# A graph layer in three turns a chunk, with its join in the same block

## The chip, the cores and the metric

The kernel runs on 1 core of a Trainium2 chip. The metric is the device time of one execution in microseconds (us); lower is better.

## The reference, cut to what matters

The program is four graph layers behind one another, each with a residual and a layer norm, over 50,000 nodes and 50,000 edges of 128 numbers. The change touches the first layer alone:

```python
def _L0_gnn_ref(x, edge_index, W, b, ln_gamma, ln_beta):
    h = x @ W
    loops = jnp.arange(N, dtype=edge_index.dtype)
    src = jnp.concatenate([edge_index[0], loops])
    dst = jnp.concatenate([edge_index[1], loops])
    deg = jax.ops.segment_sum(jnp.ones(src.shape, dtype=h.dtype), dst, num_segments=N)
    dinv = jnp.where(deg > 0, jax.lax.rsqrt(deg), 0.0)
    norm = dinv[src] * dinv[dst]
    out = jax.ops.segment_sum(h[src] * norm[:, None], dst, num_segments=N) + b
    mu = out.mean(axis=-1, keepdims=True)
    var = out.var(axis=-1, keepdims=True)
    out = (out - mu) * jax.lax.rsqrt(var + LN_EPS) * ln_gamma + ln_beta
    return jax.nn.relu(out)

x = _layernorm(x + _L0_gnn_ref(x, edge_index, ...), axis=-1)
```

## The kernel before, in words

The edges are sorted by their target. The first layer, `gcn` (L1407), takes them in 56 chunks (`k.NB`) of 7 columns (J) by 128 partitions. A chunk's tiles lie in rings: 8 slots (UB) for what is loaded and gathered, 4 (RING) for what is computed. The 7 columns go through TensorE in two groups, (0,4) and (4,7). All 56 chunks are unrolled. What is done for a chunk:

- SyncE loads the chunk's record (L1031): node and source indices, weights. `bring` (L1429) loads the source rows of the first few chunks and places words beside rows of a table.
- GpSimd, `fetch` (L1437): 14 indirect gathers, `own` (the node's own row, L1449) and `both` (the source row with two words, L1453; L1451 for the first few chunks), column by column.
- ScalarE, `weigh` (L1455): for each column one activation of the source row into `run` (L1466) and one of the own row into `summed` (L1467).
- VectorE, `edges` (L1470): 7 steps of a running sum over edges with one target (L1476), which sets `edged`; then 7 steps that add it to the own rows (L1478), which sets `prepped`.
- SyncE, `keep` (L1482): the running sums and the source words go to memory.
- TensorE: transposes (L1068); ScalarE copies (L1109); product with the folded weight (L1074 with the bias, L1080); ScalarE copies to `z` (L1117).
- VectorE, `stats` of z (L781 to L784, L777); ScalarE, logarithm and exponent, `log` (L791, L793); VectorE, `root` (L800 to L804); ScalarE, `first.apply` (L812, y<-z).
- VectorE, `residual` (L1499): scale, bias, relu and own row in three wide steps (L1502 to L1504), which sets `freed`, the release of the chunk's slot; then the second norm's stats. Then second log, second root, and on ScalarE `apply` and `apply_twice` (L812, out<-y): two normalised outputs. The latter's end is `finished`.
- SyncE, store (L1042 to L1046): both outputs to memory.

`Flow.run` (L1007) walks over turns u = −5 to 58 and gives each engine a hand-written list of (lag, stage):

- VectorE: edges of chunk u+3, stats of u, residual of u−1, first root of u, second root of u−1.
- ScalarE: copy of one group, weigh u+4, second apply (both outputs) u−2, copy of one group; then first log u, second log u−1, first apply u, copies.
- SyncE: load u+5 (waits for `freed` of the chunk 8 earlier), keep u+1 (waits for `edged`), store u−3 (waits for `finished`). So the load of chunk c stands behind the store of c−9.
- GpSimd: the gathers of one chunk after another, each chunk as soon as its record is there and its source words of 8 chunks earlier are kept.

Behind the last turn the block ends. A second block (L1541 to L1591) joins the running sums across the 128 partitions: GpSimd clears and gathers three small tiles, TensorE joins and transposes, one row per partition goes through the product and three small norms (`RowNorm`, L1168: VectorE, with GpSimd's power at L1185), and two scatters write the rows. The next stage begins with a table load on ScalarE (L2083).

Of the kernel before, what the change touches and what calls it, by code (L numbers as in the profile page):

```python
# [17 lines left out]
D = 128  # L18
J = 7
# [37 lines left out]
def wait(eng, sem, value, passed=None):  # L57

    if isinstance(value, int) and value <= 0:
        return  # L60
    eng.wait_ge(sem, value)
    if passed is not None and not isinstance(value, int):
        eng.sem_inc(passed, 1)


class Chain:
# [5 lines left out]
    def at(self, chunk):  # L72
        self.base, self.n = chunk * self.per, 0
# [1091 lines left out]
class RowNorm:  # L1165
# [7 lines left out]
        self.asked, self.rooted = k.semaphore(f"row_asked{i}"), k.semaphore(f"row_rooted{i}")  # L1173

    def run(self, dve, step, v, o):
        step(dve.bn_stats(out=self.raw[:], in_=v))
        step(dve.bn_aggr(out=self.mv[:], in_=self.raw[:]))
        step(dve.tensor_scalar(self.mv[:, 1:2], self.mv[:, 1:2], self.eps, None, ALU.add))
        dve.nop().then_inc(self.asked, 1)
        dve.wait_ge(self.rooted, 1)  # L1180
        step(dve.tensor_scalar(o, v, self.mv[:, 0:1], self.mv[:, 1:2], ALU.subtract, ALU.mult))

# [224 lines left out]
def gcn(k):  # L1407
# [3 lines left out]
    with ExitStack() as c:  # L1411
# [43 lines left out]
        def weigh(act, c):  # L1455

            i = c.slot(UB)
            if plain(c):
                act.wait_ge(xs_in[i], (c.use(UB) + 1) * 16)
            n.wait_got(act, c)  # L1460
            n.wait_rec(act, c)
            wait(act, edged, c.count(1, 2 - RING))
            wait(act, put_out[c.slot(RING)], c.use(RING) * 16)
            wait(act, n.turned, c.count(NG, (1 - RING) * NG))
            for j in range(J):
                act.activation(R(run, c)[:, j, :], xs[:, i, j, :], ACT.Copy, scale=where[:, i, j, 1:2])  # L1466
                ins = act.activation(R(summed, c)[:, j, :], own[:, i, j, :], ACT.Copy, scale=n.field(c, OWN2)[:, j : j + 1])  # L1467
            ins.then_inc(weighted, 1)

        def edges(dve, step, c):  # L1470

            r = c.slot(RING)
            dve.wait_ge(weighted, c.count(1, 1))
            for j in range(J):
                prev = run[:, r, j - 1, :] if j else run[:, (r - 1) % RING, J - 1, :]
                step(dve.scalar_tensor_tensor(run[:, r, j, :], prev, n.field(c, SAME)[:, j : j + 1], run[:, r, j, :], ALU.mult, ALU.add))  # L1476
            dve.nop().then_inc(edged, 1)
            step(*[dve.scalar_tensor_tensor(summed[:, r, j, :], run[:, r, j, :], n.field(c, OWN1)[:, j : j + 1], summed[:, r, j, :],  # L1478
                                            ALU.mult, ALU.add) for j in range(J)])
            dve.nop().then_inc(n.prepped, 1)  # L1480

        def keep(sp, c):  # L1482

# [5 lines left out]
        def kept(sp):  # L1489
            for u in range(RING):  # L1490
                sp.wait_ge(put_out[u], k.NB // RING * 16)
            for u in range(UB):
                sp.wait_ge(src_out[u], k.TN * 16)

        def stats(dve, step, c):
            n.wait_z(dve, c)
# [8 lines left out]
            dve.nop().then_inc(n.freed, 1)  # L1505
            second.stats(dve, step, c, v)

        def apply_second(act, c):
            n.wait_stored(act, c)
            act.wait_ge(src_out[c.slot(UB)], (c.use(UB) + 1) * 16)  # L1510
            second.apply(act, c, R(y, c), R(n.o[0], c))
            second.apply_twice(act, c, R(y, c), R(n.o[1], c))

        side = Prepare(k, c, [n.p_t[0][0], n.p_t[1][0], *n.p_m], [y, n.z, n.o[0]])

        def begin(dve):
            side.vector(dve)
            step = Chain(dve, begun)
            step(dve.memset(run[:, RING - 1, J - 1, :], 0.0))

            step(dve.memset(n.o[1][:, :, :, 0:1], 1.0))

        n.z_free = first.applied
        n.finished, n.freed = second.applied2, sem("freed")
        n.n_got = 2
        cut = 1
        n.run([], [], [k.res, k.tab[1]], lambda c: [R(summed, c)], [k.w_skip],
              [(3, edges), (0, stats), (-1, residual), (0, first.root), (-1, second.root)],
              [(4, weigh), (-2, apply_second), (0, first.log), (-1, second.log), (0, lambda act, c: first.apply(act, c, R(n.z, c), R(y, c)))],
              [], prep=True, sp_stages=[(1, keep)], begin=begin, sp_end=kept,  # L1530
              pe_begin=side.tensor, sp_after={-4: side.bring, UB - 1: side.put_away}, fetch=fetch, bring=bring, cut=cut)
# [5 lines left out]
        cleared, fetched, joined, done, summed1 = [sem(x) for x in ("cleared", "fetched", "joined", "jdone", "summed1")]  # L1537
        turned1, copied1, made1, ready, put = [sem(x) for x in ("turned1", "copied1", "made1", "ready", "put")]
        p_j, p_t, p_z = n.p_t[0][0], n.p_t[1][0], n.p_m[0]
        dinv = hint[:, 1:2]  # L1540
        with nc.Block(no_gpsimd_drain=True) as b:  # L1541

            @b.gpsimd
            def _(pool):
                pool.memset(head[:], 0.0).then_inc(cleared, 1)
                pool.wait_ge(cleared, 1)
                pool.indirect_dma_start(head[:], None, k.runs, bass.IndirectOffsetOnAxis(ap=k.join_row[:], axis=0),
                                        bounds_check=k.NR - 1, oob_is_err=False).then_inc(fetched, 16)
                pool.indirect_dma_start(mine[:], None, A["x"], bass.IndirectOffsetOnAxis(ap=k.head_node[:], axis=0)).then_inc(fetched, 16)
                pool.indirect_dma_start(hint[:].bitcast(I32), None, k.info, bass.IndirectOffsetOnAxis(ap=k.head_node[:], axis=0)).then_inc(fetched, 16)  # L1550
                for norm in norms:
                    norm.root(pool)
                pool.wait_ge(ready, 1)
                for table, tile in ((k.res, z), (k.tab[1], o)):
# [5 lines left out]
            def _(pe):  # L1560
                pe.matmul(p_j[:, 0:D], k.join_t[:], run[:, RING - 1, J - 1, :], start=True, stop=True).then_inc(joined, 1)
                pe.wait_ge(summed1, 1)
                pe.transpose(p_t[:, 0:D], o[:], k.ident[:]).then_inc(turned1, 1)
                pe.matmul(p_z[:, 0:D], k.ones_bf[:], k.b_rows[:, 0, :], start=True, stop=False)
                pe.wait_ge(copied1, 1)
                pe.matmul(p_z[:, 0:D], ot[:], k.w_skip[:], start=False, stop=True).then_inc(made1, 1)

            @b.scalar
            def _(act):
                act.wait_ge(turned1, 1)  # L1570
                act.activation(ot[:], p_t[:, 0:D], ACT.Copy).then_inc(copied1, 1)

            @b.vector
            def _(dve):
                step = Chain(dve, done)
                dve.wait_ge(fetched, 48)
                step(dve.tensor_scalar(o[:], mine[:], dinv, None, ALU.mult))
                dve.wait_ge(joined, 1)
                step(dve.tensor_tensor(o[:], o[:], p_j[:, 0:D], ALU.add))
                step(dve.tensor_tensor(o[:], o[:], head[:], ALU.add))  # L1580
                step(dve.tensor_scalar(o[:], o[:], dinv, None, ALU.mult))
                dve.nop().then_inc(summed1, 1)
                dve.wait_ge(made1, 1)
                norms[0].run(dve, step, p_z[:, 0:D], z[:])
# [180 lines left out]
class RowPieceNorm:  # L1765
# [1516 lines left out]
```

## Time and profile before

| | us |
|---|---|
| median of 3 runs | 7949.5 (7933.11 to 7982.95) |
| the profiled execution | 7911.97 |
| its span, first to last instruction | 7910.2 |
| busy: PE / DVE / ACT / POOL | 5034.4 / 5379.6 / 4770.6 / 3828.5 |

The span holds four layers. The first layer's chunks lie between 516 and 1867 us. PE is TensorE, DVE VectorE, ACT ScalarE, POOL GpSimd, SPq SyncE's DMA queue. In the timelines the first number is the start, the second the duration; what stands in brackets is how long the engine was idle before and what ended that.

### The profile page before, as it was taken

Reading aid. Unit: us, or ns where it says so; the run is one execution under the profiler, and the core shown is the slowest. Engines: PE = TensorE matmul, PEld = TensorE weight load, DVE = VectorE, ACT = ScalarE, POOL = GpSimd, SP = SyncE. Lnnn points to the kernel's source line nnn. Section 1 sums busy time; section 2 is a strip of 40 time slices with the busy share of each in tenths; the row PEclk is TensorE's granted clock in tenths of the full one; section 3 lists DMA queues with packets and bytes.
Section 4 is the critical chain, followed back from the end, with each engine's and each line's share of the span. In section 5 each row is a group of like instructions: output and inputs, shape, how many; then the busy total and the mean of one; then the engine's idle time right before and its main releaser. Section 6 shows DMA issues by size and latency. Waiting matters only on the chain. (4 is left out here: it accounts for less than half of the span.)

```text
span 7910.2 us, 117580 instructions
## 1 busy us (share of the span) xinstructions
PE 5034.4 (64%) x28601; PEld 3898.2 (49%) x28601; DVE 5379.6 (68%) x27204; ACT 4770.6 (60%) x14264; POOL 3828.5 (48%) x3878
## 2 busy tenths in 40 slices
PE   4032222223888886878867888865787758777774
PEld 1021111122776674666756666653454546555553
DVE  7835556564777774777766887883555777777788
ACT  6025666563677684767766777782333556666665
POOL 3055555543555534444435445425553444655565
PEclk9555555555889897998888888887888989888887
DMA  9284444433566653444434555553443883333332
GB/s 176 30 49 104 96 105 97 95 96 103 166 180 181 172 164 111 145 145 151 149 129 123 165 161 157 164 144 119 144 152 119 288 272 112 120 118 118 121 126 75
DMA packets 608007, 1075.90 MB, mean 136 GB/s; under 512 B 263700, under 2 KB 370015, under 8 KB 607193
## 3 DMA queue, kind: packets, MB, share of 16 engines
q1 hardware_dynamic: 476056, 787.63, 31.8%
q0 software_dynamic: 129920, 280.46, 16.8%
q8 instruction: 231, 3.78, 0.2%
q14 instruction: 456, 3.73, 0.2%
q10 hardware_dynamic: 1344, 0.30, 0.0%
HBM read 564.38 MB, written 530.59 MB: 138 GB/s over the span
## 5 line engine op out<-in xcount | busy, mean ns | idle before, releaser
L1975 POOL DMA_INDIRECT xs<-tab,rec x1176 | 1177.5, 1001 | 700.7 <-DVE cA L2191 412.2
L2191 DVE CUSTOM_DVE_ANT_0 junk<-p_y,xs 128x129 f32<-128x129 f32 x2352 | 586.0, 286 | 716.8 <-PE p_y L2030 248.6
L2026 PE MATMUL p_a<-w_all,xt 128*128 128x128 f32 x2352 | 545.6, 316 | 493.1 <-ACT xt L2092 322.0
L2030 PE MATMUL p_y<-w_all,xt 128*128 128x258 f32 x2352 | 796.6, 424 | 91.2 <-DMA got<-in_x,idx 35.9
L2109 ACT ACTIVATE z<-p_a 128x384 f32<-128x384 f32 x1176 | 574.6, 489 | 411.1 <-PE p_a L1866 245.7
L2101 ACT ACTIVATE st<-xs,cb 128x128 f32<-128x128 f32 x2352 | 810.0, 398 | 4.4 <-DMA xsrc<-got 4.0
L2226 DVE SCALAR_TENSOR_TENSOR st<-st,cg 128x128 f32<-128x128 f32 x2352 | 717.1, 346 | 126.6 <-ACT st L2101 74.3
L2092 ACT ACTIVATE xt<-p_t 128x256 f32<-128x256 f32 (+1 forms) x1221 | 450.0, 369 | 571.1 <-DMA both<-x_info,rec 228.6
L1449 POOL DMA_INDIRECT in<-in_x,rec x392 | 380.3, 970 | 768.9 <-DMA rec<-meta 652.7
L1074 PE MATMUL p_m<-b_rows,ones_bf 3*128 3x512 bf16 x224 | 102.8, 459 | 947.9 <-issue 397.8
L2026 PEld LDWEIGHTS p_a<-w_all,xt 128*128 128x128 f32 x2352 | 386.6, 207 | 602.6 <-ACT xt L2092 403.6
L1973 POOL DMA_INDIRECT xd<-tab,rec x336 | 336.9, 1003 | 616.3 <-DMA rec<-meta 432.6
L2846 POOL DMA_INDIRECT xs<-res,rec x392 | 386.2, 985 | 446.7 <-PE p_t L2871 183.8
L1870 PE MATMUL p_m<-w_all,z 128*128 128x128 f32 x2352 | 500.6, 297 | 77.8 <-issue 48.8
L1142 POOL DMA_INDIRECT in<-tab,rec x392 | 400.3, 1021 | 304.2 <-DMA rec<-meta 191.4
L2047 PE MATMUL p_m<-w_all,xt 128*128 128x128 f32 x2352 | 522.8, 306 | 0.0
L1074 PEld LDWEIGHTS p_m<-b_rows,ones_bf 3*128 3x128 bf16 x224 | 21.3, 95 | 1014.0 <-issue 434.5
L887 ACT ACTIVATE o<-y,norm 128x127 f32<-128x127 f32 (+1 forms) x1176 | 512.2, 486 | 6.8 <-DVE norm L881 6.6
L1871 PE MATMUL p_m<-w_all,z 128*128 128x128 f32 x2352 | 487.9, 291 | 0.0
L1866 PE MATMUL p_a<-ident,st 128*128 128x128 f32 x2352 | 484.7, 290 | 4.2 <-DVE st L2226 2.3
L2849 POOL DMA_INDIRECT out<-o,nodes x392 | 407.9, 1040 | 158.3 <-issue 117.7
L2030 PEld LDWEIGHTS p_y<-w_all,xt 128*128 128x128 f32 x2352 | 400.3, 213 | 108.7 <-issue 101.8
(784 smaller groups left out, 16742.9 us busy)
## 6 DMA issues: line engine op xcount, KB each, us to landing
states<-st SPq DMA_DIRECT2D x168, 910.0 KB
own<-tab SPq DMA_DIRECT2D x168, 448.0 KB
tab<-o SPq DMA_DIRECT2D x168, 448.0 KB
runs<-run SPq DMA_DIRECT2D x112, 448.0 KB
tab<-out SPq DMA_DIRECT2D x112, 448.0 KB
x<-tab SPq DMA_DIRECT2D x112, 448.0 KB
xd<-tab SPq DMA_DIRECT2D x168, 192.0 KB
angles<-st SPq DMA_DIRECT2D x56, 532.0 KB
```

Source lines behind the costliest of these rows:

```text
L887: ins = act.activation(o[:, r, skip:], v[:, r, skip:], ACT.Identity, bias=s[:, 1, r : r + 1], scale=s[:, 0, r : r + 1])
L1866: ins = pe.transpose(p_a[i][:, h * D : (h + 1) * D], halves(a)[:, h, :], k.ident[:])
L1870: pe.matmul(out_, a[:, 0:D], k.w_val[:, 0, :], start=False, stop=False)
L1871: return pe.matmul(out_, a[:, D : 2 * D], k.w_val[:, 1, :], start=False, stop=final)
L1975: pool.indirect_dma_start(xs[:, i, j, 0:D], None, table, bass.IndirectOffsetOnAxis(ap=rec[:, i, SRC, j : j + 1], axis=0)).then_inc(got_in[ ...
L2026: ins = pe.matmul(p_a[two(own_c, own_i)][:, 2 * D : 3 * D], xt[:, four(c, i), D : 2 * D], k.w_own[:, D : 2 * D], start=True, stop=True)
L2030: ins = pe.matmul(p_y[two(c, i)][:, 0 : H * X1], xt[:, four(c, i), 0:D], k.w_qk[:], start=True, stop=True)
L2047: pe.matmul(out_, xt[:, (four(c, j) + SCORE * J + 1) % 4, D : 2 * D], k.w_own[:, 0:D], start=False, stop=False)
L2101: ins = act.activation(state_of(r, j)[:, h, :], xs[:, c.slot(UB), j, 0:D], ACT.Copy, scale=co.b[:, c.slot(2), h, j : j + 1])
L2109: act.activation(z[:, c.slot(2), j, :], p_a[two(c, j)][:, 0 : 3 * D], ACT.Copy).then_inc(st_copied, 1)
L2191: ins = dve.tensor_tensor_reduce(junk[:, two(c, j), h], p_y[two(c, j)][:, h * X1 : (h + 1) * X1], xs[:, c.slot(UB), j, :], scale, 0.0, ALU ...
L2226: ins = dve.scalar_tensor_tensor(mine[:, h, :], prev[:, h, :], co.g[:, c.slot(2), h, j : j + 1], mine[:, h, :], ALU.mult, ALU.add)
```

## The change

The first layer is no longer run by `Flow.run`; its lists stand in `gcn`. Chunk i takes three turns: VectorE does edges, stats and first root of i in turn i, and residual and second root of i−1 in it; ScalarE does second apply of i−2. `weigh` is split: source rows first, then the logarithm of the first norm of i−1, then own rows (`weigh_own`). `edges` goes group by group, and sets `prepped` for each. SyncE loads i+5, keeps i, stores i−2. The join moves into the same block: GpSimd's small gathers go behind the last chunk's, VectorE's join arithmetic stands between the last first root and the last residual. `RowNorm.run` becomes `ask` and `take`.

```diff
+        def weigh_own(act, c):
+            for j in range(J):
+                ins = act.activation(R(summed, c)[:, j, :], own[:, c.slot(UB), j, :], ACT.Copy, scale=n.field(c, OWN2)[:, j : j + 1])
+            ins.then_inc(own_weighted, 1)
...
         def edges(dve, step, c):
...
+            for a, z_ in GROUPS:
+                for j in range(a, z_):
+                    prev = run[:, r, j - 1, :] if j else run[:, (r - 1) % RING, J - 1, :]
+                    step(dve.scalar_tensor_tensor(run[:, r, j, :], prev, n.field(c, SAME)[:, j : j + 1], run[:, r, j, :], ALU.mult, ALU.add))
+                if z_ == J:
+                    dve.nop().then_inc(edged, 1)
+                if a == 0:
+                    dve.wait_ge(own_weighted, c.count(1, 1))
+                step(*[dve.scalar_tensor_tensor(summed[:, r, j, :], run[:, r, j, :], n.field(c, OWN1)[:, j : j + 1], summed[:, r, j, :],
+                                                ALU.mult, ALU.add) for j in range(a, z_)])
+                dve.nop().then_inc(n.prepped, 1)
...
+            @b.sync
+            def _(sp):
...
+                for i in range(k.NB + 2):
+                    if i + LEAD < k.NB:
+                        load(at(i + LEAD))
+                    if i < k.NB:
+                        keep(sp, at(i))
+                    if i == UB - 1:
+                        side.put_away(sp)
+                    if i >= 2:
+                        store(at(i - 2))
...
             @b.gpsimd
             def _(pool):
+                for i in range(k.NB):
+                    fetch(pool, at(i))
                 pool.memset(head[:], 0.0).then_inc(cleared, 1)
+                pool.indirect_dma_start(mine[:], None, A["x"], ...).then_inc(hinted, 16)
+                pool.indirect_dma_start(hint[:].bitcast(I32), None, k.info, ...).then_inc(hinted, 16)
                 pool.wait_ge(cleared, 1)
+                for u in range(RING):
+                    pool.wait_ge(put_out[u], k.NB // RING * 16)
...
             @b.tensor
             def _(pe):
...
+                for i in range(k.NB):
+                    for g in range(NG):
+                        turn(at(i), g)
+                    for g in range(NG):
+                        product(at(i), g)
...
             @b.scalar
             def _(act):
...
+                for i in range(k.NB + 2):
+                    c0, c1, c2 = at(i), at(i - 1), at(i - 2)
+                    if c0.there:
+                        weigh(act, c0)
+                    if c1.there:
+                        first.log(act, c1)
+                    if c0.there:
+                        weigh_own(act, c0)
+                    if c1.there:
+                        first.apply(act, c1, R(n.z, c1), R(y, c1))
+                    if c0.there:
+                        carry_turned(c0, 0)
+                    if c2.there:
+                        n.wait_stored(act, c2)
+                        act.wait_ge(src_out[c2.slot(UB)], (c2.use(UB) + 1) * 16)
+                        second.apply(act, c2, R(y, c2), R(n.o[0], c2))
+                    if c0.there:
+                        carry_turned(c0, 1)
+                    if i == k.NB:
+                        act.wait_ge(turned1, 1)
+                        act.activation(ot[:], p_t[:, 0:D], ACT.Copy).then_inc(copied1, 1)
+                    if c2.there:
+                        second.apply_twice(act, c2, R(y, c2), R(n.o[1], c2))
+                    if c0.there:
+                        for g in range(NG):
+                            carry_product(c0, g)
+                    if c1.there:
+                        second.log(act, c1)
...
             @b.vector
             def _(dve):
...
+                for i in range(k.NB):
+                    c0, c1 = at(i), at(i - 1)
+                    stage(s_edges, c0, edges)
+                    stage(s_residual, c1, residual)
+                    stage(s_stats, c0, stats)
+                    stage(s_second, c1, second.root)
+                    stage(s_first, c0, first.root)
```

## Rows read from the trace of the kernel before

**Rows 1.** The page's chain of work that ended last, share of the span
```profile
DVE 7%; PE 4%; ACT 2%; another core or an unknown queue 2%; issue 1%; POOL 0%; DMA 0%; SPq 0%; DVEq 0%; ACTq 0%; POOLq 0%
```
**Rows 2.** Timeline: VectorE's first edges, the join block, the next stage's start
```profile
516.30 2.68 DVE L1476 SCALAR_TENSOR_TENSOR run<-run,rec 128x128 f32<-128x128 f32 x7
...
1842.01 0.43 SPq L1045 DMA_DIRECT2D tab<-out  x1
1845.92 0.20 POOL L1545 MEMSET head<- 128x128 f32 x1 [114.38 <-POOLq L1022]
...
1862.36 1.05 POOL L1555 DMA_INDIRECT res<-z,join_row  x1 [1.39 <-DVEq L1591]
...
1867.41 1.28 ACT L2083 ACT_TABLE_LOAD   x1 [13.41 <-PEq L124]
```
**Rows 3.** Waits from 600 to 1700: us in total, times, longest
```profile
POOL in L1449 <- DMA rec<-meta: 285.2, 33, 18.0
...
ACT guess L793 <- DMA xsrc<-got: 67.8, 19, 4.7
```
**Rows 4.** Timeline of SyncE's queue, stores of the first output
```profile
600.63 0.32 SPq L1045 DMA_DIRECT2D res<-out  x1
...
1160.78 0.32 SPq L1045 DMA_DIRECT2D res<-out  x1
...
1177.61 0.32 SPq L1045 DMA_DIRECT2D res<-out  x1
...
1305.45 0.32 SPq L1045 DMA_DIRECT2D res<-out  x1
...
1326.73 0.32 SPq L1045 DMA_DIRECT2D res<-out  x1
...
1707.45 0.32 SPq L1045 DMA_DIRECT2D res<-out  x1
```
**Rows 5.** Timeline of VectorE, one turn after GpSimd's last gather
```profile
1769.72 0.17 DVE L800 TENSOR_TENSOR newton<-guess 128x14 f32<-128x14 f32 x1 [0.33 <-DVE norm L804]
...
1771.08 2.68 DVE L1476 SCALAR_TENSOR_TENSOR run<-run,rec 128x128 f32<-128x128 f32 x7 [0.34 <-DVE norm L804]
...
1776.15 1.45 DVE L781 BATCH_NORM_STATS2 raw<-z 128x6 f32<-128x128 f32 x7 [0.33 <-DVE summed L1478]
...
1778.82 1.09 DVE L1502 TENSOR_TENSOR y<-y,ln_g 128x896 f32<-128x896 f32 x1 [0.33 <-DVE rad L777]
...
1785.06 0.17 DVE L800 TENSOR_TENSOR newton<-guess 128x7 f32<-128x7 f32 x1 [0.33 <-DVE rad L904]
...
1786.36 0.17 DVE L800 TENSOR_TENSOR newton<-guess 128x14 f32<-128x14 f32 x1 [0.33 <-DVE norm L804]
```
**Rows 6.** Timeline of GpSimd, first and last of 28 gathers
```profile
1164.91 0.95 POOL L1449 DMA_INDIRECT in<-in_x,rec  x1 [5.04 <-DMA rec<-meta]
...
1199.69 0.94 POOL L1453 DMA_INDIRECT both<-x_info,rec  x1 [0.30 <-issue]
```
**Rows 7.** Stretch: us; busy PE, PEld, DVE, ACT, POOL; clock, DMA share, GB/s
```profile
1179.00:1204.00 25.00, 5.30 (x22) 4.17 (x21) 4.28 (x24) 10.10 (x30) 16.45 (x18) 0.50 0.48 98
```
**Rows 8.** Timeline of ScalarE in that stretch
```profile
1195.24 0.39 ACT L1466 ACTIVATE run<-both 128x128 f32<-128x128 f32 x1
...
1200.79 0.49 ACT L812 ACTIVATE out<-y,norm 128x128 f32<-128x128 f32 x1 [0.98 <-issue]
```
**Rows 9.** Waits of SyncE's queue from 600 to 1700
```profile
SPq L1031 <- DVEq L1505: 67.1, 14, 9.5
```
**Rows 10.** Groups by shape, 600 to 1700: busy us, mean ns, idle before
```profile
L1068 PE MATMUL p_t<-ident,summed 128*128 128x128 f32 x322 | 87.6, 420 | 0.0
```
**Rows 11.** Timeline of ScalarE, the undisturbed turn of rows 5
```profile
1772.56 0.47 ACT L1109 ACTIVATE xt<-p_t 128x384 f32<-128x384 f32 x1
1772.93 5.48 ACT L812 ACTIVATE out<-y,norm 128x128 f32<-128x128 f32 x14
...
1784.81 0.21 ACT L791 ACTIVATE guess<-rad 128x14 f32<-128x14 f32 x1 [5.11 <-DVEq L785]
```

More of the change, by code:

```diff
@@ L1175, in run, with ask @@
     def run(self, dve, step, v, o):
+        self.ask(dve, step, v)
+        self.take(dve, step, v, o)
+    def ask(self, dve, step, v):
         step(dve.bn_stats(out=self.raw[:], in_=v))
@@ L1179, in run, with take @@
         dve.nop().then_inc(self.asked, 1)
+    def take(self, dve, step, v, o):
         dve.wait_ge(self.rooted, 1)
@@ L1465, in weigh @@
             for j in range(J):
-                act.activation(R(run, c)[:, j, :], xs[:, i, j, :], ACT.Copy, scale=where[:, i, j, 1:2])
-                ins = act.activation(R(summed, c)[:, j, :], own[:, i, j, :], ACT.Copy, scale=n.field(c, OWN2)[:, j : j + 1])
+                ins = act.activation(R(run, c)[:, j, :], xs[:, i, j, :], ACT.Copy, scale=where[:, i, j, 1:2])
             ins.then_inc(weighted, 1)
+        def weigh_own(act, c):
+            for j in range(J):
+                ins = act.activation(R(summed, c)[:, j, :], own[:, c.slot(UB), j, :], ACT.Copy, scale=n.field(c, OWN2)[:, j : j + 1])
+            ins.then_inc(own_weighted, 1)
         def edges(dve, step, c):
@@ L1473, in edges @@
             dve.wait_ge(weighted, c.count(1, 1))
[L1474 to L1480, printed above, removed]
+            for a, z_ in GROUPS:
[9 more added lines that the diff above has]
+                dve.nop().then_inc(n.prepped, 1)
         def keep(sp, c):
@@ L1506, in residual @@
             second.stats(dve, step, c, v)
[L1508 to L1512, printed above, removed]
-        side = Prepare(k, c, [n.p_t[0][0], n.p_t[1][0], *n.p_m], [y, n.z, n.o[0]])
[L1516 to L1521, printed above, removed]
+        side = Prepare(k, c, [n.p_t[0][0], n.p_t[1][0], *n.p_m], [y, n.z, n.o[0]])
         n.z_free = first.applied
         n.finished, n.freed = second.applied2, sem("freed")
[L1525 to L1531, printed above, removed]
+        n.n_got, n.n_out = 2, 2
+        outs = [k.res, k.tab[1]]
+        at = lambda i: Chunk(k, i // UB, i % UB)
         head, mine, hint, o, ot, z = [sb(x, s) for x, s in (("head", [P, D]), ("mine", [P, D]), ("hint", [P, 2]), ("o", [P, D]),
@@ L1536, in gcn @@
         norms = [RowNorm(k, c, i) for i in range(3)]
-        cleared, fetched, joined, done, summed1 = [sem(x) for x in ("cleared", "fetched", "joined", "jdone", "summed1")]
+        own_weighted = sem("own_weighted")
+        cleared, hinted, fetched, joined, done, summed1 = [sem(x) for x in ("cleared", "hinted", "fetched", "joined", "jdone", "summed1")]
         turned1, copied1, made1, ready, put = [sem(x) for x in ("turned1", "copied1", "made1", "ready", "put")]
-        p_j, p_t, p_z = n.p_t[0][0], n.p_t[1][0], n.p_m[0]
+        p_j, p_t, p_z = side.sets[1][0:3]
@@ L1540, in gcn, with load, store @@
         dinv = hint[:, 1:2]
         with nc.Block(no_gpsimd_drain=True) as b:
+            @b.sync
+            def _(sp):
+                def load(c):
+                    wait(sp, n.freed, c.count(1, 1 - UB), n.passed)
+                    sp.dma_start(n.rec[:, c.slot(UB)].rearrange("p f j -> p (f j)"),
+                                 k.meta[:, c.n].rearrange("p f j -> p (f j)")).then_inc(n.rec_in[c.slot(UB)], 16)
+                    bring(sp, c)
+                def store(c):
+                    wait(sp, n.finished, c.count(1, 1), n.passed)
+                    for i, table in enumerate(outs):
+                        sp.dma_start(rows(table)[:, c.n, :],
+                                     n.o[i][:, c.slot(RING)].rearrange("p j d -> p (j d)")).then_inc(n.stored[c.slot(RING)], 16)
+                for i in range(LEAD):
+                    load(at(i))
+                    if i == 1:
+                        side.bring(sp)
+                for i in range(k.NB + 2):
[8 more added lines that the diff above has]
+                for u in range(RING):
+                    sp.wait_ge(n.stored[u], k.NB // RING * 16 * n.n_out)
+                    sp.wait_ge(put_out[u], k.NB // RING * 16)
+                for u in range(UB):
+                    sp.wait_ge(src_out[u], k.TN * 16)
@@ L1543, in _ @@
             @b.gpsimd
             def _(pool):
+                for i in range(k.NB):
+                    fetch(pool, at(i))
                 pool.memset(head[:], 0.0).then_inc(cleared, 1)
+                pool.indirect_dma_start(mine[:], None, A["x"], bass.IndirectOffsetOnAxis(ap=k.head_node[:], axis=0)).then_inc(hinted, 16)
+                pool.indirect_dma_start(hint[:].bitcast(I32), None, k.info, bass.IndirectOffsetOnAxis(ap=k.head_node[:], axis=0)).then_inc(hinted, 16)
                 pool.wait_ge(cleared, 1)
+                for u in range(RING):
+                    pool.wait_ge(put_out[u], k.NB // RING * 16)
@@ L1553, in _ @@
                 pool.wait_ge(ready, 1)
+                for u in range(RING):
+                    pool.wait_ge(n.stored[u], k.NB // RING * 16 * n.n_out)
                 for table, tile in ((k.res, z), (k.tab[1], o)):
@@ L1560, in _, with turn, product @@
             def _(pe):
+                def turn(c, g):
+                    a, z_ = GROUPS[g]
+                    pe.wait_ge(n.prepped, c.count(NG, g + 1))
+                    wait(pe, n.copied, c.count(NG, g - 1))
+                    for r in range(a, z_):
+                        ins = pe.transpose(n.p_t[g][0][:, (r - a) * D : (r - a + 1) * D], R(summed, c)[:, r, :], k.ident[:])
+                    ins.then_inc(n.turned, 1)
+                def product(c, g):
+                    a, z_ = GROUPS[g]
+                    wait(pe, n.z_in, c.count(NG, g - 1))
+                    pe.matmul(n.p_m[g][:, 0 : (z_ - a) * D], k.ones_bf[:], k.b_rows[:, 0 : z_ - a, :].rearrange("p r d -> p (r d)"),
+                              start=True, stop=False)
+                    pe.wait_ge(n.copied, c.count(NG, g + 1))
+                    for r in range(z_ - a):
+                        ins = pe.matmul(n.p_m[g][:, r * D : (r + 1) * D], n.xt[:, g, 0, r * D : (r + 1) * D], k.w_skip[:], start=False,
+                                        stop=r == z_ - a - 1)
+                    ins.then_inc(n.made, 1)
+                side.tensor(pe)
+                for i in range(k.NB):
[3 more added lines that the diff above has]
+                        product(at(i), g)
+                pe.wait_ge(edged, k.NB)
                 pe.matmul(p_j[:, 0:D], k.join_t[:], run[:, RING - 1, J - 1, :], start=True, stop=True).then_inc(joined, 1)
+                pe.matmul(p_z[:, 0:D], k.ones_bf[:], k.b_rows[:, 0, :], start=True, stop=False)
                 pe.wait_ge(summed1, 1)
                 pe.transpose(p_t[:, 0:D], o[:], k.ident[:]).then_inc(turned1, 1)
-                pe.matmul(p_z[:, 0:D], k.ones_bf[:], k.b_rows[:, 0, :], start=True, stop=False)
                 pe.wait_ge(copied1, 1)
@@ new lines, in carry_product @@
+                def carry_product(c, g):
+                    a, z_ = GROUPS[g]
+                    act.wait_ge(n.made, c.count(NG, g + 1))
+                    if g == 0:
+                        wait(act, n.z_free, c.count(1, 1 - RING))
+                    act.activation(n.z[:, c.slot(RING), a:z_, :].rearrange("p j d -> p (j d)"),
+                                   n.p_m[g][:, 0 : (z_ - a) * D], ACT.Copy).then_inc(n.z_in, 1)
+                for i in range(k.NB + 2):
[26 more added lines that the diff above has]
+                        second.log(act, c1)
@@ L1573, in _, with stage @@
             @b.vector
             def _(dve):
+                side.vector(dve)
+                begin = Chain(dve, begun)
+                begin(dve.memset(run[:, RING - 1, J - 1, :], 0.0))
+                begin(dve.memset(n.o[1][:, :, :, 0:1], 1.0))
+                s_edges, s_residual, s_stats, s_second, s_first = [
+                    Steps(dve, sem(x), n.passed) for x in ("d_edges", "d_residual", "d_stats", "d_second", "d_first")]
+                def stage(step, c, what):
+                    if c.there:
+                        step.at(c)
+                        what(dve, step, c)
+                        step.end()
@@ L1582, in _ @@
                 dve.nop().then_inc(summed1, 1)
+                stage(s_residual, final, residual)
                 dve.wait_ge(made1, 1)
-                norms[0].run(dve, step, p_z[:, 0:D], z[:])
+                norms[0].ask(dve, step, p_z[:, 0:D])
+                stage(s_second, final, second.root)
+                norms[0].take(dve, step, p_z[:, 0:D], z[:])
                 step(dve.tensor_tensor(z[:], z[:], k.ln_g[:], ALU.mult))
```

19 lines of the change are left out of this document (9 added, 10 removed).

## The prediction

> **What bounds the kernel now.** The chain of waits comes first: it is shared out thinly, VectorE leading with 7% [rows 1], so no single engine is the answer and the stage has to be read by itself. The change touches only the first layer, which runs from about 516 us (when VectorE is done with the weights) to 1867.41, where the next stage's table load starts [rows 2].
>
> The waits of that stretch show GpSimd idle 285.2 us for the record of the next chunk [rows 3]. It is not short of time: it waits for a load that stands in SyncE's queue right behind a store. So I read SyncE's stores next [rows 4]. From 600.63 to 1707.45 lie 46 turns, 24.06 us each, but they are not alike: 16.83 from 1160.78 on, 21.28 from 1305.45 on, and others must be far longer.
>
> What would a turn cost without disturbance? After GpSimd's last gather VectorE goes from second root to second root in 16.64 us (1769.72 to 1786.36), without a pause longer than 0.34: second root and its hand-over 1.36, edges 5.07, stats 2.67, residual 6.24, first root 1.30 [rows 5]. There the turn is VectorE's. The other 7.4 us come with GpSimd's gathers.
>
> GpSimd's rows show it: 28 gathers without a pause from 1164.91 to 1200.63, 1.28 each, so 17.5 to 18 a chunk [rows 6]. From 1179 to 1204, while this run lasts, VectorE is busy 4.28 of 25 us and ScalarE 10.10 [rows 7]. ScalarE shows what a slow stretch looks like: 14 weighings begin at 1195.24 and are over before 1200.79, under 0.4 us each, and there one row of 0.49 us stands behind 0.98 us of nothing [rows 8]. Of the 38 unbroken runs of gathers in the stage 25 are one chunk long and 13 two. A run of one chunk costs the others little, some 3.6 us at its tail, where ScalarE's second step of the logarithm stands (67.8 in 19 cases [rows 3]); a run of two costs the 25 us of that window. I take it that about 14 us of unbroken gathering sets the slow stretch off and a pause ends it; the trace shows the order in time, not the cause.
>
> Whether two chunks run together is a race. A store at 1160.78 lets GpSimd start at 1164.91, 4.13 later; the next store at 1177.61 is 12.7 into that run, its load lands before the run ends, and the runs join. The store at 1326.73 followed its forerunner by 21.28, so it came some 17 into its run: it was itself held until the run was nearly over, and the runs stayed apart.
>
> **The change, part by part.**
> *Loads and stores.* Today load c stands behind store c−9 and waits for the release of slot c−8; that wait cost 67.1 us in 14 cases, 4.8 each [rows 9]. In the new order load c stands behind store c−8, whose chunk has released its slot long before. The wait goes: 67.1/46 = −1.46 a turn at most. What is late next is the gather itself: it starts earlier, which can make two runs join where the wait kept them apart. Keep moves one place as well: SyncE's keep of the running sums now waits for the edges of the same turn, and behind it stand the store and the next load; these wait for the second apply, later in the same turn, so it holds up nothing.
>
> *VectorE's turn.* Same operations. Edges go in two groups, each with its own hand-over: between nothing and two pauses of the 0.34 that stand ahead of edges, 0.68; I take 0.36, so 17.0 a turn [rows 5].
>
> *The chain across the engines.* It now closes within one turn, where the old order gave it five. From the start s of edges: the first four columns are ready at s+2.9 (8 of 14 steps of 5.07), PE's four transposes at 0.42 [rows 10] take 1.3 to 1.7, ScalarE copies 0.5, applies the second norm once (7 rows, half of 5.48) 2.7, copies 0.5, applies it again 2.7 [rows 11]: the chunk two back is finished at s+10.8. Two more copies make z ready at s+11.7. VectorE's edges and residual take 5.4 + 6.2, so it gets there at s+11.7 as well: between nothing and 0.6 us of new wait for z, I take 0.3. A turn is 17.3, 0.66 over today's floor. Own rows are weighed in the second half of the old weighing, 2.0 us, while VectorE does first root and the first four run steps: hidden. ScalarE today waits 5.11 for stats in the undisturbed turn [rows 11]; this slack pays for the new waits. If the cover of the own rows is gone, the turn gets up to 2.0 longer. The first logarithm moves between the two weighings, just as stats end: nothing either way, up to 0.5.
>
> *GpSimd* has the same 14 gathers a chunk. *The start:* the first store comes in turn 2: 516 + 2×17.3 + 10.8 = 561, plus one slow stretch while GpSimd rushes: 15 (0 to 24); I take 576.
>
> *The end and the join.* Today 160 us lie between the store at 1707.45 and the next stage; the join block alone starts at 1845.92 [rows 2]. New: 47 turns behind the first store the last load goes out; then a turn with gathers (24), five at the floor (86), the drain of the last chunk: 6.3 to the end of first root, 2.7 apply, 6.2 residual, 1.9 logarithm and root, 5.4 second apply = 22.5. The join's own arithmetic and its two gathers lie beside that. What stays behind the last store: its landing, 3.9 (1842.01 to 1845.92), and the two scatters to the next stage, 5.05 (1862.36 to 1867.41), so 9 at least; 13 with the queues in between. If the join's cover were gone it would cost its 16 us again (1845.92 to 1862.36). Sum 145, against 160.
>
> *Sum:* the next stage starts at 576 + 47T + 145 = 721 + 47T, T the mean turn under gathers. Even with today's 1867.4 at T = 24.4. The sum hangs on T.
>
> *T.* 24.06 today, −1.46 for the release, +0.66 for the floor, and a loss in the slow stretches: ScalarE could run 14 weighings ahead there (from 1195.24 on), some 4 us of work for later turns; in the new order it can weigh only half of it before it needs VectorE, which is the slowest. 4 over three turns is 1.3; between 0 and that, 0.7. T = 24.0.
>
> 721 + 47×24.0 = 1849: −18 us. The profiled run had 7911.97 (span 7910.2), the median of three is 7949.5; the 18 us are taken from the median: **7931 us**.
>
> **The Trainium skill against the rows.** "SBUF — State Buffer", section "Who interferes with whom", says that a DMA never contends with a compute engine and that ScalarE's ports are shared with nobody. By it the gathers could not slow ScalarE, and the stalls would come from waits in the old order; the time would be that of rival C. Rows 8 speak against it, as ScalarE shows pauses there that no engine's release ends. No row shows which resource is short.
>
> **The rivals.**
> *A, runs stay apart:* the store comes 14 us or more into each run, is held to its end, and the next run starts afresh. For: the floor rises by 0.66, and ScalarE's in-order list makes the chunk finish late in the turn; s+10.8 plus 4.1 gives a run start, and the next finish is 17.3 − 4.1 = 13.2 in, only 0.8 short. It is self-holding: each tail costs some 4 us, so the next finish is late as well. Against: 13.2 is below 14. A turn is then 21.3 (1305.45 to 1326.73): 721 + 47×21.3 = 1722, −145: 7804.
>
> *B, slower:* every run joins with the next, in pairs, as no release wait parts them, and the tight chain advances in the slow stretch only as fast as VectorE, 4.28 of 25 us. From the store at 1177.61 to the stretch are 1.4 us, and it ends at 1204, 3.4 behind the run: 17.3 − 1.4 − 4.3 = 11.6 of the turn are left then, so the store comes 15.0 behind the run and the next run 4.1 later. Pair: 35.7 + 15.0 + 4.1 = 54.8, T = 27.4, +141: 8091. With ScalarE's 10.10 in place of 4.28 it is 49.0, T = 24.5, and nothing is lost. It decides from T = 26.1 (under 6.9 us get through); between that and 27.4 I take 26.7, +108: 8058. For: 13.2 lies near the 12.7 at which runs joined. Against: GpSimd restarted late after each pair today, and a single run followed.
>
> *C, no slow stretches:* T is the gathers' own 17.5: 721 + 823 = 1544, −324: 7626. Only if their cause is the order of the old queue.
>
> *D, the change brings only the end:* T stays at 24.06 because release, floor and lost advance cancel. 1852, −15: 7934. It is the forecast's neighbour and shares its chance.
>
> **How the numbers follow.** 1% is 79 us, about what a measurement of this kernel can tell from no change. Forecast with D, T from 22.7 to 26.1: 0.42 (range by itself 7870 to 8029). A 0.32, C 0.04: faster 0.36. B 0.22. The mixture can settle between A and B, so the range takes A with a margin down to T = 20.8 (7780) and B up to 26.7 (8058, rounded to 8060); left out are C and the outer halves of B and a few cases of A, 0.2.
>
> **What would show it.** Right: gather runs of 35 us still alternating with runs of 17 to 18, the release wait behind the record's load gone, VectorE's undisturbed turn 17.0 to 17.6 with a short wait for z before stats, the next stage's table load some 145 us behind the store that frees the last load. A: nearly all runs single and turns of 20.5 to 22. B: hardly a single run, two stores every 52 us or more. Wrong: an undisturbed turn over 18 (the chain, not VectorE, would be the bound), slow stretches under single runs, or a join that stands alone behind the last store.

## The result, and the profile after

The changed kernel is slower: 8050.14 us median (8031.36 to 8056.98, 4 runs) against 7941.31 (7912.96 to 7982.95, 4 runs) beside it, ratio 1.0144, interval 1.0111 to 1.0177. The forecast was 18 us shorter; it came out 109 us longer, as rival B had it. That B's +108 is met so closely is partly luck: only 81 us of the difference lie in the edited layer, as the next lines show.

The profiled executions differ by 119.5 us (spans 8029.7 and 7910.2). 81.3 of these lie in the first layer, whose end is the next stage's table load: 1948.71, before 1867.41 [rows 2]. The other 38 lie in stages that were not edited; the kernel before differs by 70 us between its own four runs, so no cause is given for them here. By the three terms of the sum:

| | forecast | before | after |
|---|---|---|---|
| first store | 576 | 600.63 | 597.05 |
| mean of the next 47 turns | 24.0 | 24.08 | 25.72 |
| from that store to the next stage | 145 | 135.0 | 142.9 |
| next stage starts | 1849 | 1867.4 | 1948.7 |

The turn makes +77, the end +8, the start −4. SyncE's stores and loads in the timeline of the changed kernel show what became of the turn:

```profile
1149.33 0.32 SPq L1546 DMA_DIRECT2D res<-out  x1
...
1166.57 0.32 SPq L1546 DMA_DIRECT2D res<-out  x1
...
1203.77 0.32 SPq L1546 DMA_DIRECT2D res<-out  x1
...
1220.73 0.32 SPq L1546 DMA_DIRECT2D res<-out  x1
```

Turns of 17.2, 37.2 and 17.0: that is the pattern nearly throughout. GpSimd's gathers in the same stretch, the first of a run, the last of it, and the first of the next:

```profile
1153.41 0.94 POOL L1455 DMA_INDIRECT in<-in_x,rec  x1 [17.85 <-DMA rec<-meta]
...
1187.86 0.94 POOL L1459 DMA_INDIRECT both<-x_info,rec  x1 [0.30 <-issue]
...
1208.40 0.94 POOL L1455 DMA_INDIRECT in<-in_x,rec  x1 [19.61 <-DMA rec<-meta]
```

The run begins 4.1 behind the store at 1149.33. The next store comes 13.2 into it, its load lands as the first chunk's gathers end (a pause of 0.68), and the run goes on to 1188.80: 35.4 us, two chunks. The stores then stop until 1203.77, and GpSimd restarts 4.6 later: 55.0 us for two chunks, where rival B had 54.8. Behind the pair the turn is 17.0 again (1220.73), 12.3 into the new run, so that one is joined as well.

Not every pair is gathered without a break. Behind the opening there are 12 unbroken runs of two chunks and 26 of one, where the kernel before had 13 and 25. But 11 pairs of the single runs are only 0.7 to 2.1 us apart, and behind ten of these eleven comes a turn of 30 us or more, just as behind an unbroken run. Counted in this way the changed kernel has 23 pairs, the kernel before 14 (13 unbroken, one with a pause of 0.9). In this text two chunks are joined when no more than some 2 us part them.

What a turn is worth without and within a slow stretch, by the busy time of the engines (us; PE, PEld, DVE, ACT, POOL) in two stretches of the changed kernel:

```profile
1168.00:1192.00 24.00, 0.00 (x0) 0.00 (x0) 3.53 (x23) 5.38 (x19) 15.55 (x17) 0.55 0.30 85
1193.00:1210.00 17.00, 6.57 (x23) 4.55 (x23) 14.21 (x61) 14.99 (x43) 1.29 (x2) 0.50 0.25 84
```

In 24 us TensorE does nothing and VectorE 3.53 us of work; five us behind the run a whole turn takes 17. ScalarE no longer gets ahead there: 5.38 busy, before 10.10 [rows 7]. Not all of this idle time is of one kind:

```profile
1165.14 1.65 PE L1607 MATMUL p_m<-w_all,xt 128*128 128x128 f32 x6
...
1177.35 0.49 ACT L1641 ACTIVATE z<-p_m 128x384 f32<-128x384 f32 x1 [10.33 <-DMA idx<-in_src]
...
1187.84 0.23 DVE L804 SCALAR_TENSOR_TENSOR norm<-mean,norm 128x14 f32<-128x14 f32 x1 [1.23 <-issue]
...
1196.25 1.11 PE L1597 MATMUL p_t<-ident,summed 128*128 128x128 f32 x4 [29.46 <-DVEq L1495]
```

ScalarE stands 10.33 us although the product that it copies ended at 1166.79; the transfer that the profile names as the releaser started in the first 7 us of the execution. VectorE's small steps then follow one another with pauses of mostly 1.2 to 1.9 us for which the profile names no other engine, and ScalarE waits 8.41 us for them. TensorE only waits for VectorE's edges, so its zero does not show that it is slowed itself.

VectorE's undisturbed turn in the timeline (edges, stats, second root, first root, next edges) answers to [rows 5]:

```profile
1193.45 1.52 DVE L1488 SCALAR_TENSOR_TENSOR run<-run,rec 128x128 f32<-128x128 f32 x4 [0.34 <-DVE norm L804]
...
1198.76 1.09 DVE L1511 TENSOR_TENSOR y<-y,ln_g 128x896 f32<-128x896 f32 x1 [0.33 <-DVE summed L1493]
...
1204.99 1.46 DVE L781 BATCH_NORM_STATS2 raw<-z 128x6 f32<-128x128 f32 x7 [0.33 <-DVE rad L904]
...
1207.66 0.17 DVE L800 TENSOR_TENSOR newton<-guess 128x14 f32<-128x14 f32 x1 [0.33 <-DVE rad L777]
...
1209.01 0.17 DVE L800 TENSOR_TENSOR newton<-guess 128x7 f32<-128x7 f32 x1 [0.33 <-DVE norm L804]
...
1210.40 1.51 DVE L1488 SCALAR_TENSOR_TENSOR run<-run,rec 128x128 f32<-128x128 f32 x4 [0.34 <-DVE norm L804]
```

16.95 from edges to edges, with no pause for z. Edges take 5.31, before 5.07: the second group costs 0.24.

SyncE's waits from 600 to 1700, all of some size: the release wait of [rows 9] is gone, and keep now waits for edges.

```profile
SPq L1500 <- DVEq L1490: 567.6, 26, 31.1
SPq L1546 <- ACT out L812: 126.8, 24, 6.8
```

The first edges start at 534.40, 18 us later than before [rows 2], and the last store, the scatters and the next stage follow one another as forecast:

```profile
534.40 1.51 DVE L1488 SCALAR_TENSOR_TENSOR run<-run,rec 128x128 f32<-128x128 f32 x4
...
1939.14 0.32 SPq L1546 DMA_DIRECT2D res<-out  x1
...
1943.64 1.06 POOL L1586 DMA_INDIRECT res<-z,join_row  x1 [5.41 <-DMA tab<-out]
...
1948.71 1.28 ACT L2209 ACT_TABLE_LOAD   x1 [9.60 <-PEq L124]
```

### The profile page after: what moved, and what is told of

Its sections match the earlier page's. It is cut to its first block and busy times, and to the rows that moved or that the text cites. A ratio compares the mean times of both kernels' runs of the same rounds, so it can differ in the third digit from the quotient of the medians.

```text
span 8029.7 us, 117738 instructions
## 1 busy us (share of the span) xinstructions
PE 5080.1 (63%) x28601; PEld 3918.6 (49%) x28601; DVE 5384.2 (67%) x27204; ACT 4773.6 (59%) x14264; POOL 3811.8 (47%) x3878
## 5 line engine op out<-in xcount | busy, mean ns | idle before, releaser
L1597 PE MATMUL p_t<-ident,summed 128*128 128x128 f32 x392 | 113.0, 437 | 1019.6 <-DVEq L1495 777.2
L1597 PEld LDWEIGHTS p_t<-ident,summed 128*128 128x128 f32 x392 | 68.2, 215 | 1058.1 <-DVEq L1495 793.7
```

## The experiments

Theory J: two chunks gathered in one run cost the time, and whether runs join is a race of the next store against the run. Theory C: the chain closed within three turns is slow by itself. Times are medians in us; they are compared with the kernel before on the same chip, since its own median was 8043, 8040 and 7955 on the three chips used.

**a_noown: fewer gathers.**
```diff
-                pool.indirect_dma_start(own[:, i, j, :], None, A["x"], mine).then_inc(n.got[i], 16)
...
+                    sp.dma_start(own[:, c.slot(UB)].rearrange("p j d -> p (j d)"),
+                                 A["x"][0 : P * J, :].rearrange("(p j) d -> p (j d)", p=P)).then_inc(own_in[c.slot(UB)], 16)
```


> The changed kernel without the gather of own rows: each chunk loads the same 896 rows of x in one plain load instead, so 7 gathers a chunk are left out. J: runs of 9 us, far under the onset, a pause behind each; no slow stretch, every turn 16.9 to 17.3 as behind the last gather, first layer 350 to 410 us shorter, time 7640 to 7720. C: turn 20 or more even so. If the stores or plain loads make the slow stretch, it stays, as there are more of them.

The kernel leaves out the gathers of the chunks' own rows. 7579.2 in its one run. The mean turn is 17.02, nearly all of the turns 16.9 to 17.5; the runs are 8.4 to 9.4 us long. The stores, 16.87 and 16.96 apart:

```profile
1093.49 0.32 SPq L1548 DMA_DIRECT2D res<-out  x1
1110.36 0.32 SPq L1548 DMA_DIRECT2D res<-out  x1
1127.32 0.32 SPq L1548 DMA_DIRECT2D res<-out  x1
```

The closed chain runs at its floor, then; C falls as far as the chain is concerned. The time is lower than expected, since the first store comes at 515.2 as well, 82 earlier, of which 29.5 are VectorE's first edges (504.90): the opening, too, had been slowed.

**a_slow and a_slow1: more work in each turn.** Two idle multiplications (a_slow1: one) behind first root.
```diff
+                    stage(s_idle, c0, lambda dve, step, c: [step(dve.tensor_tensor(idle[:], idle[:], idle[:], ALU.mult)) for _ in range(2)])
```


> The changed kernel with 2.2 us of idle work (two wide multiplications of a tile nobody reads) at the end of each of VectorE's turns. Theory J (race): the undisturbed turn goes from 16.95 to 19.2, so the next store comes 19.2 - 4.5 = 14.7 into a run in place of 12.4, is caught by the slow stretch and held; runs stay single, mean turn from 25.7 down to 20.5 to 22, time 150 to 230 us SHORTER than the changed kernel, though each turn has more work. Theory C (the tight chain or VectorE's work sets the turn): 2.2 us more each turn, 100 to 125 us longer.

7970.55 (8 runs), against 8107.76 for the unaltered changed kernel on that chip (a_again): 137 us shorter with 2.2 us more work a turn, a little less than the 150 expected at least. Mean turn 22.62, where 20.5 to 22 was expected; behind the opening one run of 49 has two chunks. The timeline shows a run's start, the idle work, the store held to the end of the run (1306.21 + 17.7), and the next run's start:

```profile
1306.21 0.94 POOL L1455 DMA_INDIRECT in<-in_x,rec  x1 [3.48 <-DMA rec<-meta]
...
1311.74 2.22 DVE L1699 TENSOR_TENSOR idle<-idle 128x896 f32<-128x896 f32 x2 [0.33 <-issue]
...
1324.52 0.32 SPq L1547 DMA_DIRECT2D res<-out  x1
...
1330.21 0.94 POOL L1455 DMA_INDIRECT in<-in_x,rec  x1 [6.28 <-DMA rec<-meta]
```

This is the race of J, shown by the one number that C and J move in opposite ways: the stores behind the opening come 14.8 to 18.3 into a run, in the changed kernel mostly 12.1 to 13.4.

> The changed kernel with 1.1 us of idle work a turn, half of a_slow's. J: the next store comes 18.1 - 4.5 = 13.6 into a run, at the edge (runs joined at 12.4, stayed apart at 14.7): some pairs left, mean turn 22.5 to 25.5, between the changed kernel and a_slow. C: 50 to 60 us longer than the changed kernel.

7872.12, 0.9915 (0.9887 to 0.9944) of the kernel before; mean turn 22.27, again one run of two chunks behind the opening. Half the idle work parts nearly as many runs: only five turns of 30 or more are left, three of them in the opening, and the mean lies just under the 22.5 expected at least. Further on, the two stores at 13.9 into a run leave pauses of 1.0 and 1.3 and a turn of 30 to 31 behind them. One at 14.0 leaves 1.4 and no such turn, and neither do those from 14.2 on, whose pauses are 2.1 or more. So the edge lies near 14.

**b_order: the change's order of load and store alone, in the kernel before.** The store goes ahead of the load in `one`.
```diff
                 def one(t, u):
+                    if self.store_first:
+                        put(t, u)
                     c = chunk(t, u, LEAD)
...
-                    c = chunk(t, u, -DRAIN)
-                    if c.there:
...
```


> The kernel before with one thing of the change: SyncE stores ahead of the load, so that the load of a chunk stands behind the store of the chunk 8 earlier and no longer waits for a release. If the release wait was what parted the runs: nearly all runs joined, mean turn 25 to 26.5, 50 to 110 us longer than the kernel before. If the closed chain of the change is what joins them (the loose old chain takes 22 to 27 us for the turn behind a pair whatever the load does): runs as before, double and single in turn, mean turn 22.5 to 24, the same or up to 70 us shorter.

8020.12, ratio 0.9969 (0.9939 to 0.9999): 20 us shorter. Mean turn 23.82; 11 of the 40 runs behind the opening have two chunks, with turns of 24 between the pairs. So the release wait was not what parted the runs; taking it away costs nothing, and the gain is at the edge of the noise.

**a_end, a_half, b_end, b_end_again: a pause between gathers.**
```diff
             for j in range(J):
...
+            pool.wait_ge(n.got[i], (c.use(UB) + 1) * 16 * 2 * J)
```
a_half has the wait behind columns 4 and 7:
```diff
+                if j == 3 or j == J - 1:
+                    pool.wait_ge(n.got[i], c.use(UB) * 16 * 2 * J + (j + 1) * 32)
```


> The changed kernel, with one wait added: GpSimd waits for the rows of a chunk to land before it gathers the next chunk. Theory J (two chunks gathered in one run cost the turn; the release wait that parted some of them is gone): hardly a run of gathers over 18 us, mean turn under gathers from 25.7 down to 20 to 22, median 7800 to 7880. Theory C (the chain closed within three turns is slow by itself, whatever GpSimd does): turn stays at 24 to 26 and the time within 1% of the changed kernel's 8050. If landing takes as long as the slow stretch did, also 24 or more, but then with single runs.

7926.25, ratio to the kernel before 0.9856 (0.9781 to 0.9931). No run is over 18.2 us, yet the mean turn is 24.13 and turns of 18 and 32 still alternate in the first half, where the pause between the two chunks of most pairs was 1.7 to 2.2; near the end, with pauses mostly of 2.5 and more, most turns are 21 to 22. A pause of that length doesn't end the slow stretch, so "hardly a long run" was too weak a condition. About half of its gain over the changed kernel is in the opening, where the first store came at 515.0.

> The changed kernel; GpSimd waits for its rows to land twice a chunk, after column 4 and after column 7. J with an onset after some 14 us of unbroken gathering: no run over 9 us, no slow stretch at all, turn is 17.5 of gathers plus two landings of 2 to 4 us, 21.5 to 25.5, median 7850 to 8030. C: no change, 8050. If the slow stretch comes with the mere amount gathered and not with its being unbroken, VectorE and ScalarE show pauses over 1 us between instructions all the same.

7948.24, ratio 0.9903 (0.987 to 0.9936). Mean turn 23.85, from the seventh on all alike (23.3 to 25.7), and no slow stretch. Busy time in two of its turns:

```profile
1184.00:1208.00 24.00, 6.50 (x23) 4.55 (x23) 14.32 (x60) 14.55 (x43) 13.09 (x15) 0.57 0.39 98
1208.00:1232.00 24.00, 6.56 (x23) 4.55 (x23) 14.14 (x60) 15.24 (x46) 13.79 (x15) 0.50 0.38 99
```

TensorE and VectorE do a whole turn in each; the rest is waiting for rows, as the waits from 600 to 1620 say, ScalarE for the gathered rows:

```profile
ACT run L1474 <- DMA both<-x_info,rec: 358.5, 42, 11.0
```

GpSimd is the bound there: 17.0 of gathers and pauses of 1.9 and some 5 for its rows to land. The kernel gathers the same rows as the changed one, so it is not the amount gathered that makes the slow stretch.

> The kernel before, with the wait of a_end. J: its 13 double runs go, mean turn from 24.1 to 20 to 22, median 100 to 190 us under the kernel before (7941), and the kernel before and the changed one come out within 60 us of each other, the changed one ahead by its shorter end. C: the kernel before hardly changes, and the changed one stays 1% or more behind it.

7884.2, ratio 0.9831 (0.9762 to 0.99): 1.7% under the kernel before. All runs single, mean turn 21.55, every turn under gathers 20.4 to 25.6. Here the pauses came out at 2.7 to 5.2 in the steady part, most of them over 3. That the changed kernel would be ahead with the same wait did not come true: a_end is 42 us behind b_end.

> b_end once more, the kernel before with the wait for landing once a chunk, beside the others on their chip: 1.2 to 2.2% under the kernel before, all runs single, turn 21.3 to 21.8.

7803.09, ratio 0.9814 (0.9765 to 0.9864), turn 21.67.

**a_gap: a longer pause in the changed kernel.**
```diff
+            pool.wait_ge(n.got[i], (c.use(UB) + 1) * 16 * 2 * J)
+            for m in range(2):
+                pool.memset(idle[:], 0.0).then_inc(idled, 1)
+                pool.wait_ge(idled, c.n * 2 + m + 1)
```


> The changed kernel; GpSimd waits for the rows of a chunk to land and then fills a tile that nobody reads twice (some 1 us each) before it gathers on. In a_end the pause was 1.9 us and the turns stayed at 24.1. J, if a pause must last some 2.5 us or more: pauses of 4 us, all runs single, mean turn 21 to 22.5 in place of 24.1, 80 to 150 us under the changed kernel by more than a_end gave. C, or if the pause's length is not what counts: turn 24 or, with 2 us more on GpSimd, 26.

7775.69, ratio 0.979 (0.9742 to 0.9837). All runs single, mean turn 21.97, in place of a_end's 24.13, with 2 us more for GpSimd to do. The pause in the timeline, landing and filling:

```profile
1315.14 1.75 POOL L1462 MEMSET idle<- 128x896 f32 x2 [2.70 <-DMA both<-x_info,rec]
...
1336.94 1.75 POOL L1462 MEMSET idle<- 128x896 f32 x2 [1.70 <-DMA both<-x_info,rec]
```

Pauses of 3.5 and more part the chunks where 1.9 did not. Between the two the runs differ: 2.1 to 2.9 were enough in a_slow1 behind its opening, one of 2.5 in a_again was not. This kernel, the change with the pause, is 2.1% under the kernel before on its chip, on which the change without the pause was not run. b_end_again, on the same chip, is 27 us behind it with overlapping intervals, so which of the two is better isn't settled.

**b_ten: pauses of 1.9 every ten gathers, in the kernel before.** The wait of a_half, placed behind each tenth gather.

> The kernel before; GpSimd waits for its rows to land after every tenth gather (two chunks are 28), in place of once a chunk. J with an onset at 14 us: runs of 12.5 us at most, no held stores, turn 17.5 + 1.4 x 2 = 20 to 21.5, as good as b_end or up to 70 us better. If 1.9 us of pause do not end what 12.5 us of gathering began: slow stretches again, turn 22 to 24.5.

7814.25, ratio 0.9853 (0.9797 to 0.9909), mean turn 22.51: no better than b_end. Runs of 12.2 to 13.2 us did not give the 20 to 21.5 that an onset at 14 us and any pause would have.

**a_hold: the load of chunk 5 behind the first keep, as before.**
```diff
                 for i in range(k.NB + 2):
+                    if i == 0:
+                        keep(sp, at(i))
                     if i + LEAD < k.NB:
                         load(at(i + LEAD))
-                    if i < k.NB:
+                    if 0 < i < k.NB:
                         keep(sp, at(i))
```


> The changed kernel with the load of chunk 5 behind the first keep, as in the kernel before. If the earlier load of chunk 5 lengthened the opening (gathers of 105.6 us in place of 88.3, VectorE's first edges 18 us later): first edges back at 516 and the first store some 18 us earlier; the median 10 to 25 us under the changed kernel's of the same chip, as the pairs stay. Rival (the opening is late for another reason, as a wait in the one block): first edges stay at 534.

8131.43 against 8107.76: not shorter. The cause of VectorE's late start is confirmed (first edges at 517.07, the opening run 88.0), but the first store does not follow it: 593.9 here, 581.7 in a_again, whose first edges come at 534.18. The mean turn is 26.44.

**a_again.**

> The changed kernel once more, beside the others on their chip, since the kernel before took 8043 on a second chip and 7941 on the first. J: pairs in both kernels are a matter of phase, so the medians move with the chip; the changed one 0 to 1.5% over the kernel before, mean turn 25 to 27.

8107.76 (10 runs), ratio 1.0081 (1.005 to 1.0113) to the kernel before on that chip, mean turn 25.96: five turns of 20.5 to 28.6 first, then mostly pairs of 17 and 31 to 37. The change is slower on both chips.

## Why the prediction was wrong, point by point

- *The floor.* Right. 17.3 was expected, 16.95 measured; edges cost 0.24 more (0.36 taken), and there is no wait for z.
- *The release wait.* It went as said, but its −1.46 a turn was the wrong sort of term: b_order, without it, has 23.82 in place of 24.08, 0.26.
- *The step that failed* is T, which was to change by −0.06 and changed by +1.64. I added price by price to the old mean turn (24.06 − 1.46 + 0.66 + 0.7) and so took the old mix of double and single runs for given; the line "GpSimd restarted late after each pair today, and a single run followed" was held against rival B. That single run was the old chain's doing: b_order, with the old chain and the new order of load and store, keeps its turns of 24 between the pairs. Three stores of the kernel before, the first behind a pair:

```profile
1208.26 0.32 SPq L1045 DMA_DIRECT2D res<-out  x1
...
1235.38 0.32 SPq L1045 DMA_DIRECT2D res<-out  x1
...
1251.52 0.32 SPq L1045 DMA_DIRECT2D res<-out  x1
```

  and ScalarE in the first of these turns, its wait and the chunk's two outputs:

```profile
1216.86 0.21 ACT L791 ACTIVATE guess<-rad 128x14 f32<-128x14 f32 x1 [5.79 <-DVEq L785]
...
1225.70 5.48 ACT L812 ACTIVATE out<-y,norm 128x128 f32<-128x128 f32 x14
```

  ScalarE waits 5.79 for VectorE's stats, most of which (5.11) stands in the undisturbed turn as well [rows 11], and only then weighs; it ends the outputs at 1231.18, 14.8 into the run that began at 1216.37. The store follows at 1235.38, when that run is over: the turn behind the pair took 27.1, and its store missed the run. In the changed kernel that turn is 17.0 and nearly every run is joined: 23 pairs in place of 14. The working had the number for it: 13.2 into the run (mostly 12.1 to 13.4 measured), under the 14 that I had set as the edge. From it B should have been the likeliest. The regular turn is what makes the pairs regular; a_slow, which makes each turn longer, parts them.
- *B's price* was right in its parts (a pair 54.8, measured 55.0); the mean is 25.72 and not 27.4 because most pairs are shorter (48.8 to 56.2, 52.5 in the mean) and some single turns (18.8 to 24.9) come in between in that execution. That is under the 26.1 from which B was counted, so T by itself still lies within the forecast's bounds (22.7 to 26.1); its change had the wrong sign. Where B expected hardly a single run, single runs are not rare, but most of them stand close together.
- *The start* was mis-sized: 576 for 597.05. I had left out that the load of chunk 5 moves ahead of the first keep: the opening run grows from 88.3 to 105.6 us, and VectorE's work on the weights ends 18 us later. a_hold shows this cause for VectorE's start, but not for the first store, which stayed at 593.9 without it and came at 581.7 with it in a_again. What sets the first store is open.
- *The end.* 145, measured 142.9. But it saves nothing: the 160 us I set against it began one store earlier, and from the same store the kernel before needs 135.0. Behind its last weighing it had turns of 12.5 to 13.2, where the new order still has 16.9. The join itself went as forecast: 9.6 us from the last store to the next stage, 25.8 before (1841.65 to 1867.41).
- *Rival A* (runs apart, turn 21.3) is what the changed kernel does once something parts the runs: 22.3 to 22.6 in a_slow1 and a_slow, 21.97 in a_gap. *Rival C* falls: the slow stretch is no matter of the old queue's order. It came in the new order too and went with the gathers (a_noown). The rule of the Trainium skill weighed there ("SBUF — State Buffer", section "Who interferes with whom": a DMA never contends with a compute engine) doesn't help here: where 35 us are gathered at a stretch, ScalarE stands 10.33 us with its operand ready. Whether SBUF or another resource is short, no run shows.

## What to carry to other kernels

When two streams can lock in phase, the mean turn is not a sum of old terms: work out for the new schedule where the next trigger falls in the running burst, and which state that feeds. A shorter, steadier turn can be the slower one if it meets the burst at the wrong moment; test that by adding idle work, which tells a race from a bound. A burst that slows the other engines is worth a deliberate pause in it, and the pause must be long enough: 1.9 us between chunks did not part them here, 3.5 did.

## What the runs showed of the hardware that was not expected

Long gathering by GpSimd slows ScalarE and VectorE while they have work: two chunks of 14 gathers each (35 us) leave VectorE 3.53 of 24 us busy and ScalarE 5.38, one chunk of 7 (8.4 to 9.4 us) leaves the turn at its floor. TensorE stands still with them, but as it waits for VectorE. Both how long the gathers last and how long they pause count: 17.5 us with pauses of 1.9 is slow, 9.8 and 7.2 with pauses of 1.9 and some 5 isn't. Which resource runs short was not tried; that an engine can do a dozen instructions at full speed in such a stretch when it had waited just before (ScalarE, [rows 8]) is a hint and no more. The kernel before had medians from 7941 to 8043 on the chips used; only one of its executions was traced, so the reason is open.
